# Cross-attention of sixteen heads on one core: the products with values moved to the front of each key tile, the scores of two tiles ahead to its end, and every low part made on VectorE

## What is computed

```python
def _mha(q, k, v, heads=8):
    scores = jnp.einsum('bhqd,bhkd->bhqk', qh, kh) * d ** (-0.5)
    probs = jax.nn.softmax(scores, axis=-1)
    return jnp.einsum('bhqk,bhkd->bhqd', probs, vh)

query, keyt, valt = x @ Wq, enc @ Wk, enc @ Wv   # enc: all but the last 4 context rows
hs = _mha(query, keyt, valt)
# ca_hs2: a small second attention over the last 4 context rows
out = (hs + ca_hs2) @ Wout + b_out + x
```

## Time and profile before

| | us |
|---|---|
| median of 3 runs | 1215.57 |
| lowest and highest | 1214.51, 1216.21 |
| the profiled execution | 1215.66 |
| its span, first to last instruction | 1213.8 |

### The profile page before, as it was taken

The page is one execution under the profiler, slowest core; times in us unless marked ns, Lnnn a source line. Parts: engine busy times, 40 slices in busy tenths (PEclk is TensorE's granted clock), DMA queues, the critical chain, the costliest instruction groups (busy, mean ns, idle before and its releaser), DMA issues.

```text
span 1213.8 us, 14595 instructions
## 1 busy us (share of the span) xinstructions
PE 1201.0 (99%) x5660; PEld 908.1 (75%) x5660; DVE 824.5 (68%) x1179; ACT 681.6 (56%) x784; POOL 206.0 (17%) x117
## 2 busy tenths in 40 slices
PE   7999999999999999999999999999999999999999
PEld 6888888787666667777777777777777777776899
DVE  6458625761144378888888888888888888885551
ACT  5323433223644377677777677677777777778310
POOL 0100000010000021222221221221221221221233
PEclk9999999999999999999999999999999999999999
DMA  8975785693910074254344344335335325422254
GB/s 297 347 276 174 260 298 209 232 319 120 301 16 1 1 196 98 87 132 110 98 121 110 109 120 112 106 111 126 100 102 145 96 87 153 125 73 66 70 218 148
DMA packets 77936, 178.09 MB, mean 147 GB/s; under 512 B 14169, under 2 KB 31705, under 8 KB 74026
## 3 DMA queue, kind: packets, MB, share of 16 engines
q1 hardware_dynamic: 70106, 156.29, 42.2%
q0 software_dynamic: 2864, 10.24, 2.6%
q10 hardware_dynamic: 4896, 10.62, 2.6%
HBM read 113.72 MB, written 63.24 MB: 146 GB/s over the span
## 4 chain that ended last, share of the span: by engine, by line
PE 99%; ACT 0%; DMA 0%; issue 0%; DVE 0%; ACTq 0%
PE at_ps L1281 30%; PE bank L698 20%; PE at_ps L1262 20%; PE at_ps L234 9%; PE acc_t_ps L1055 7%; PE at_ps L1469 6%; PE s_ps L1023 2%; PE bank L645 1%; PE bank L675 1%; PE f_ps L998 1%; PE acc_t_ps L1034 1%; PE f_ps L234 1%; PE f_ps L977 1%; PE f_ps L987 0%; PE at_ps L1472 0%; DMA ctx_f<-in_ctxT 0%
## 5 line engine op out<-in xcount | busy, mean ns | idle before, releaser
L250 DVE TENSOR_REDUCE mpart<-at_ps 128x1 f32<-128x512 f32 x480 | 325.3, 686 | 99.8 <-PE at_ps L234 99.7
L1202 ACT ACTIVATE prob_hi<-at_ps 128x1024 fp32r<-128x1024 f32 (+1 forms) x256 | 263.0, 1027 | 188.9 <-PE at_ps L1262 188.9
L1281 PE MATMUL at_ps<-prob_hi,v 128*81 128x512 f32 (+1 forms) x1024 | 317.1, 395 | 0.2 <-issue 0.2
L1139 DVE TENSOR_TENSOR prob_lo<-probs,prob_hi 128x1024 fp32r<-128x1024 f32 (+1 forms) x211 | 271.7, 1288 | 24.0 <-ACT probs L1207 23.4
L1207 ACT ACTIVATE probs<-at_ps 128x1024 f32<-128x1024 f32 (+1 forms) x256 | 261.3, 1021 | 0.0
L1281 PEld LDWEIGHTS at_ps<-prob_hi,v 128*81 128x81 f32 (+1 forms) x1024 | 150.5, 149 | 69.6 <-issue 6.2
L1139 POOL TENSOR_TENSOR prob_lo<-probs,prob_hi 128x1024 fp32r<-128x1024 f32 x45 | 108.0, 2401 | 514.2 <-ACT probs L1207 514.2
L234 PE MATMUL at_ps<-a 128*128 128x512 f32 x480 | 188.1, 392 | 0.0
L1262 PE MATMUL at_ps<-a 128*128 128x512 f32 (+1 forms) x512 | 160.0, 394 | 1.2 <-ACT probs L1207 0.6
L1262 PE MATMUL at_ps<-b 113*128 113x512 f32 (+1 forms) x512 | 161.1, 396 | 0.0
L1281 PE MATMUL at_ps<-prob_lo,v 128*81 128x512 f32 (+1 forms) x512 | 160.3, 394 | 0.0
(11 more groups left out here) (149 smaller groups left out, 1392.8 us busy)
## 6 DMA issues: line engine op xcount, KB each, us to landing
v_hi_d<-v_t SPq DMA_DIRECT2D x16, 648.0 KB, 5.8
v_lo_d<-v_t SPq DMA_DIRECT2D x16, 648.0 KB, 7.1
v<-v_hi_d SPq DMA_DIRECT2D x16, 648.0 KB, 4.8
v<-v_lo_d SPq DMA_DIRECT2D x16, 648.0 KB, 6.0
k_hi_d<-out_hi SPq DMA_DIRECT2D x40, 256.0 KB, 5.9
k_lo_d<-out_lo SPq DMA_DIRECT2D x40, 256.0 KB, 6.3
a<-k_hi_d SPq DMA_DIRECT2D x16, 640.0 KB, 7.6
b<-k_hi_d SPq DMA_DIRECT2D x16, 640.0 KB, 11.2
```

Of the source, the lines that this page charges most:

```text
L250: dve.tensor_reduce(self.mpart[:, g % 2, qt, c:c + 1], at[:, 0:w], AX, ALU.max).then_inc(self.mx_done, 1)
L1139: eng.tensor_tensor(pl[n % PB][0:r, :], prob[n % PF][0:r, :], ph[n % PB][0:r, :].bitcast(F32), ALU.subtract).then_inc(sem, 1)
L1202: act.activation(ph[n % PB][0:r, :], s_ps[n % 2][0:r, :], ACT.Exp, scale=SCALE).then_inc(ph_done, 1)
L1281: mm = pe.matmul(o_ps[:, u * CH:(u + 1) * CH], a[0:r, t, :], y[n % PB][0:r, u * CH:(u + 1) * CH], start=t == 0 and m == 0, stop=t == KT - ...
```

## The change

In a tile TensorE now makes `values(n)` with both pieces inside, after the first and the second pair, then `scores(n + 2)` at the end, without pieces inside and without the wait on `e_done` (the low part that `values(n)` has waited for is made after both activations that read the same PSUM pair). The row piece takes the place after the second pair, and the two pieces of that tile come one after the other behind the third pair. `SPLIT_AT` goes from 1 to 2: VectorE reduces both pieces of tile n before it makes the low part of tile n+1. `POOL_T` is empty: GpSimd makes no low part. ScalarE's order is as before.

```diff
-POOL_T = (4, 9, 14)
-SPLIT_AT = 1
+POOL_T = ()
+SPLIT_AT = 2
...
-            def scores(n, between):
+            def scores(n):
...
-                if n >= 2:
-                    pe.wait_ge(e_done, n - 1)
...
-                    if first:
-                        between()
...
-            scores(0, lambda: None)
+            scores(0)
             gathered(pe, 1)
-            scores(1, lambda: None)
+            scores(1)
...
-                if n + 2 < N:
-                    scores(n + 2, between)
                 values(n, between)
                 while todo:
                     between()
+                if n + 2 < N:
+                    scores(n + 2)
```

## The result

| | before | changed |
|---|---|---|
| median, us | 1215.24 (4 runs) | 1302.93 (4 runs) |
| lowest and highest | 1214.51, 1216.21 | 1302.41, 1305.69 |
| span of the profiled execution | 1213.8 | 1300.6 |
| mean granted TensorE clock | 1.000 | 0.980 |

The ratio is 1.0724, with a 95% interval from 1.0711 to 1.0738: 7.2% slower, 87.7 us. The prediction was 1279.5 us with a range of 1265 to 1297. The direction and both large terms were right, the size was not: 23 us are missing, and the mean clock says where to look.

A forecast was written before the change was run, and what follows sets the result against it. TensorE's own pace was taken as the bound. Net 31.1 at changes of head, 27.7 and 0.2 for the row, 2.7 last head, 1.5 start, 0.6 GpSimd: 63.8 us on 1215.66 gives 1279.5, range 1265 to 1297.

The forecast's parts named there:

- both large terms: TensorE's waits for `take` at 15 changes of head, 33.7 us, and for the row's copy in tile 12, 27.7 us.
- The common tile: Ordinary attention tiles: the low part ends 0.65 us before its product needs it, so the tile stays at 2.79 us.
- The change of head: Next head's first product waits for `take`, behind a later activation on ScalarE: 2.25 us, 15 times, 33.7 us.
- the old loss: TensorE's earlier waits at changes of head, 0.15 us each and some 0.4 more at the last: 2.6 us goes.
- The row piece: Tile 12: the next piece waits for the row's copy, behind a low part on VectorE: 1.98 us, 14 times, 27.7 us.
- The last head and the start: Tiles from 236 on, without pieces, lose 2.7 us; the first tiles and head 0 lose 1.5 us.
- GpSimd: Behind each reciprocal, `normalise` waits inside a low part and delays the next one: 0.04 us, 15 times, 0.6 us.
- The rival of the seam: After `normalise`, GpSimd's weight split goes ahead of the waiting low part in 9 heads: 13 us, giving 1292; chance 0.12.
- The clock: Rival: TensorE at half clock for one tile behind each of 29 gaps of about 2 us: 70 us, 1349; chance 0.04.

The follow-up runs named there:

- the run with GpSimd back: Changed kernel with the low parts of three tiles a head (45 in all) made on GpSimd again: 1325.33 us, ratio 1.0905.
- the run with the gaps filled: Changed kernel with unread matmuls in TensorE's idle time, 8 at each change of head and 7 in each tile 12: 1281.34 us.
- with the row first: Changed kernel with the row's copy and one maximum ahead of the low part on VectorE in tile 12: 1263.30 us, ratio 1.0391.
- with only tile 12 filled: Changed kernel with 7 unread matmuls in tile 12's gap only, the gap at each change of head left: 1301.39 us, ratio 1.0712.

## Why the prediction was right in its waits and wrong in its size

- **The common tile** (0 us): right. 0.65 us were to be left between a low part and its product; the pattern stands, and with GpSimd's 2.40 for 1.22 the product was late by the 1.18 of difference less these 0.65, as the run with GpSimd back shows.
- **The change of head** (2.25 us, 15 times): right. 2.46 - 0.23 = 2.23 in each, 33.5 in all. Less the 2.6 of the old loss it is 30.9 for the 31.1 of the sum.
- **The row piece** (1.98 us, 14 times): right in mechanism, a little small. The piece starts 2.11 after the one ahead, 1.88 more than the pace. The row piece itself came 0.14 late, and the released matmul, whose weights were loaded only then, held the next by 0.11 (718.85, then the scores at 719.19). Together 2.13, so 29.8 for 27.7; the kernel before had lost 0.4 at these places, which leaves 29.4.
- **The last head and the start** (2.7 + 1.5): about right. From its first product's start to its last one's the last head takes 38.87 us (1183.30 to 1222.16) for 151 steps from start to start, before 34.35 (1101.05 to 1135.40) for 147; four steps of 0.233 taken off, 3.6 are lost. At the start 1.2 are lost at the first low part, where 0.9 were lost at the scores of tile 2. Together 3.9 for 4.2.
- **GpSimd** (0.6): right in time and place, and worth nothing in 14 heads. `normalise` did come inside the low part of a tile and wait for it, but no product there came late. Only in the last head, without pieces, one came 0.96 late; it is in the 3.6 above. The rival of the seam, 0.12, did not happen: the waiting low part went first, nine times of nine.
- **The clock**: this is the step that failed. The sum had no term for it. The rival had the right mechanism, TensorE at half clock behind a gap of 2 us, but a chance of 0.04, because no row showed a fall after so short a gap. No row showed a gap of that length either: the longest idle time in the stage was 0.63 us. Nothing spoke against it, and absence was read as a no. It was also priced only as all or nothing, 70 us, so that it lay outside the range as a whole. What came were 15 falls behind 29 gaps: 21.6 us by the run with the gaps filled, 23.6 by the length of the heads. 1279.5 + 23.6 is 1303.1, for 1302.9 measured, and the run with the gaps filled gave 1281.3, near the sum without the clock.

The account: 30.9 at the changes of head, 29.4 in tile 12, 3.9 in the last head and at the start, 23.6 of clock, which makes 87.8. The medians differ by 87.7, the spans of the profiled executions by 86.8. Without the clock the terms add up to 64.2, where the prediction had 63.8.

## What to carry to other kernels

Where an engine is busy for 99% and waits for nothing, an edit to its order can hardly win. Follow instead each thing that is waited for once in many rounds (a result taken out, a row turned). It was in time only thanks to work that the edit moves elsewhere, and the edit does not change its place in the other engines' lists. A wait of TensorE can cost more than its own length: here about half of the waits of 2.1 to 2.5 us cost 1.6 more each through the clock. Put something behind which the wait fits, useful work if there is any (a matmul moved by one place brought 2 us here), else matmuls that nobody reads. And where no row shows a case, the rows say nothing against it: give it a price for a part of the places too, and not only for all of them.

## What the hardware showed that I had not expected

- Behind gaps of 2.1 to 2.6 us between matmul starts TensorE often ran 7 or 8 matmuls of 512 columns at the 1.2 GHz level (0.427 us apart) and then went back to 2.4 GHz (0.233): 12, 4 and 12 of 15 times at changes of head, in the changed kernel, with the row first and with only tile 12 filled. Behind 28 gaps of 1.40 to 1.53 us it never did so. The Trainium skill (TensorE: Matmul & The Clock Gate, "Part 1: The HAM clock gate") has this fall behind idle time; by these traces it comes behind less of it than I had taken for safe.
- The fall does not always begin with the first matmul behind the gap: a pair at full pace (0.66 us) came first at 730.65, a slow one (1.05 us) at 718.15 in the run with the row first.
- Idle time of 2.5 us can be made cheaper by filling it half: 4 useless matmuls at each change of head and 3 in each tile 12 did as much as 8 and 7, 1281.4 against 1281.3 us.
- When GpSimd's `normalise` ended and both a low part on VectorE and GpSimd's next operation were waiting, VectorE's went first, in nine heads of nine (700.64 to 702.42, and the split behind it stretched from 1.56 to 2.44 us).
